# The slots' weights of a graph kernel's last layer in a PSUM bank of their own

## The reference

```
s = x @ msg_w[:, :D].T
d = x @ msg_w[:, D:].T
messages = gelu(s[:, None, :] + d[None, :, :] + msg_b)
aggregated = einsum('ijd,ij->id', messages, adj)
new = concat([x, aggregated], -1) @ upd_w.T + upd_b
h = gelu(new) + x
out = (h - mu) / sqrt(var + eps) * ln_w + ln_b
```

## Time and profile before

| | |
|---|---|
| median of the runs | 754.19 us |
| profiled execution, first to last instruction (span; no other time of that execution is recorded) | 758.7 us |
| busy: TensorE, VectorE, ScalarE, GpSimd | 461.8, 505.2, 302.4, 376.7 us |
| the last layer's pairs | from about 448 us to the end |

### The profile page before, as it was taken

How to read it: one execution, slowest core, us unless ns; L and a number is a source line. 1 busy time by engine, 2 the same in 40 slices (tenths; PEclk the granted TensorE clock), 3 DMA queues, 4 the chain that set the end, 5 groups by cost and what they waited for, 6 DMA issues and landing times.

```text
span 758.7 us, 6873 instructions
## 1 busy us (share of the span) xinstructions
PE 461.8 (61%) x1987; PEld 273.2 (36%) x1987; DVE 505.2 (67%) x1592; ACT 302.4 (40%) x362; POOL 376.7 (50%) x499
## 2 busy tenths in 40 slices
PE   5222016999959999999994586545524642484111
PEld 4121013444425565454463464333313431342110
DVE  2509806998944547983344845999797779777744
ACT  2665255457742331898553230132323222322213
POOL 7204610766650303763003746577777777776640
PEclk9555555899989999999998569677656665655555
DMA  8999992999940202799002221111122122212200
GB/s 325 353 425 419 397 381 39 368 415 390 392 186 0 74 0 76 283 404 421 13 14 78 73 71 49 31 52 49 52 52 56 45 55 54 55 46 56 52 15 14
DMA packets 33212, 120.07 MB, mean 158 GB/s; under 512 B 8704, under 2 KB 19892, under 8 KB 24148
## 3 DMA queue, kind: packets, MB, share of 16 engines
q1 hardware_dynamic: 20258, 80.99, 27.1%
q0 software_dynamic: 10176, 38.57, 16.3%
q10 hardware_dynamic: 2734, 0.01, 0.2%
HBM read 114.00 MB, written 5.55 MB: 158 GB/s over the span
## 4 chain that ended last, share of the span: by engine, by line
PE 34%; POOL 22%; DMA 20%; issue 11%; DVE 6%; ACT 3%; another core or an unknown queue 1%; SPq 1%; ACTq 0%; POOLq 0%
PE ps L121 33%; DMA ring<-in_adjT_dram 18%; POOL G L919 17%; POOL Go L919 5%; DMA G<-near,IX 2%; ACT binT L1001 1%; PE ps L1257 1%; PE ps L1263 1%; DVE M L1703 1%; SPq L822 0%; DVE X L1696 0%; DVE E L1797 0%; ACTq L1004 0%; DVE st L1687 0%
## 5 line engine op out<-in xcount | busy, mean ns | idle before, releaser
L919 POOL DMA_INDIRECT G<-near,IX x154 | 159.6, 1036 | 58.3 <-issue 49.7
L121 PE MATMUL ps<-ring,hwu 128*128 128x512 f32 (+3 forms) x264 | 114.8, 588 | 1.0 <-ACT hwu L1014 1.0
L121 PE MATMUL ps<-ring,xT_s 128*128 128x512 f32 (+2 forms) x264 | 106.9, 547 | 2.0 <-DMA ring<-in_adjT_dram 2.0
L121 PE MATMUL ps<-ident,agg 128*128 128x128 f32 (+1 forms) x44 | 15.9, 461 | 135.6 <-DVE agg L1827 105.2
L1503 DVE FIND_INDEX8 I<-V,rows 128x8 uint32<-128x340 f32 (+2 forms) x176 | 88.1, 504 | 0.0
L1513 DVE MAX8 V<-rows 128x8 f32<-128x340 f32 (+2 forms) x176 | 85.5, 496 | 0.8
L121 PE MATMUL ps<-E,M 128*128 128x321 f32 (+2 forms) x192 | 65.6, 502 | 22.8 <-DVE IO L1719 15.3
L121 PEld LDWEIGHTS ps<-ring,hwu 128*128 128x128 f32 (+1 forms) x264 | 51.4, 204 | 64.4 <-issue 63.3
L1001 ACT ACTIVATE binT<-ring 128x2708 bf16<-128x2708 f32 (+1 forms) x22 | 53.9, 2457 | 44.1 <-DMA ring<-in_adjT_dram 44.1
L942 POOL DMA_DIRECT2D rows<-in_adj_dram x18 | 10.9, 603 | 120.6 <-DVE I L1503 120.6
L1021 ACT ACTIVATE binT<-ring 128x2708 bf16<-128x2708 f32 (+1 forms) x22 | 54.0, 2456 | 37.5 <-PE ps L121 28.4
(11 more groups left out here) (255 smaller groups left out, 859.1 us busy)
## 6 DMA issues: line engine op xcount, KB each, us to landing
ring<-in_adjT_dram SPq DMA_DIRECT2D x48, 1354.0 KB, 16.9
rows<-in_adj_dram POOLq DMA_DIRECT2D x17, 1354.0 KB, 10.2
rows<-in_adj_dram SPq DMA_DIRECT2D x4, 1354.0 KB, 23.4
G<-near,IX POOLq DMA_INDIRECT x154
xT_s<-in_xT_dram SPq DMA_DIRECT2D x1, 1354.0 KB, 6.6
near<-hwu SPq DMA_DIRECT2D x1, 1344.0 KB
out_dram<-yo SPq DMA_DIRECT2D x21, 64.0 KB
near2f<-hwu SPq DMA_DIRECT2D x5, 256.0 KB
```

The source lines that it names most:

```text
L121: return pe.matmul(dst, lhsT, rhs, start=start, stop=stop, skip_group_check=True)
L919: pool.indirect_dma_start(out=dst, out_offset=None, in_=table, in_offset=bass.IndirectOffsetOnAxis(ap=index, axis=0), engine_sem=o_g).then ...
```

## The change

The weights `T8` are copied once by ScalarE, before the pairs begin, into PSUM bank 2, and the multiply in `aggregate` reads them there. Bank 2 held the own shares of every third pair; these now take turns on banks 0 and 1. The share of pair g+1 is made in pair g (from g = 1), at the place in TensorE's order at which that of g+2 stood. The first two shares are made ahead of the pairs, as before. It waits for `features(g-1)`, the last reader of its bank, which is the same wait (`c_h` at g in pair g) as before.

```
--- before.py
+++ after.py
@@ -42,6 +42,7 @@
 MSLOTS = 10
 SUMS = 7 - CAP
 LEAD3 = 3
+SLOT_BANK = 2
 
 
 PAIRS = 11
@@ -258,6 +259,7 @@
         acc = ps[:, 6 * BANK:6 * BANK + D]
         trn = ps[:, 6 * BANK + D:6 * BANK + 2 * D]
         prj = ps[:, 7 * BANK:8 * BANK]
+        slot_weights = bank(SLOT_BANK, 0, NB * 8).rearrange("p (n k) -> p n k", k=8)
         list_bank = ps[:, (8 - CAP) * BANK:8 * BANK].rearrange("p (k e) -> p k e", e=BANK)
         threes = [(q, min(3, GP - q)) for q in range(0, GP, 3)]
 
@@ -290,6 +292,7 @@
         c_hw, c_sg, c_w, c_hws, c_zs = sem("c_hw"), sem("c_sg"), sem("c_w"), sem("c_hws"), sem("c_zs")
         c_acc, c_std, c_x, c_xT, c_hw1, c_pr = sem("c_acc"), sem("c_std"), sem("c_x"), sem("c_xT"), sem("c_hw1"), sem("c_pr")
         c_neg, c_dinv, c_d = sem("c_neg"), sem("c_dinv"), sem("c_d")
+        c_slots = sem("c_slots")
         c_msg, c_msgo, c_aggS, c_h = sem("c_msg"), sem("c_msgo"), sem("c_aggS"), sem("c_h")
 
         v_few, v_set, v_wa, v_u3, v_w2a, v_e, v_w3 = (sem("v_few"), sem("v_set"), sem("v_wa"), sem("v_u3"), sem("v_w2a"),
@@ -1140,6 +1143,9 @@
                 act.activation(pd3[0:r, b, 0:D], bank(g % 2, 0, count * D)[0:r, :].rearrange("p (q w) -> p q w", w=D),
                                ACT.Copy).then_inc(c_d, 1)
 
+            act.wait_ge(v_win, 1)
+            act.activation(slot_weights, T8[:, :, :], ACT.Copy).then_inc(c_slots, 1)
+
             def messages(n):
                 act.wait_ge(v_pre, n + 1)
                 at = G3[0:rn(n), n % QUEUE3, :, :]
@@ -1159,7 +1165,7 @@
                 act.wait_ge(p_nf, g + 1)
                 if g:
                     act.wait_ge(v_h, g)
-                act.activation(hh[:, :, :], bank(g % 3).rearrange("p (b w) -> p b w", w=2 * D)[:, :, D:2 * D], ACT.Gelu).then_inc(c_h, 1)
+                act.activation(hh[:, :, :], bank(g % 2).rearrange("p (b w) -> p b w", w=2 * D)[:, :, D:2 * D], ACT.Gelu).then_inc(c_h, 1)
 
             def deviations3(g, first=0, last=2):
                 for k in range(first, last):
@@ -1394,14 +1400,14 @@
 
             def own_shares(g):
 
-                if g >= 3:
-                    pe.wait_ge(c_h, g - 2)
+                if g >= 2:
+                    pe.wait_ge(c_h, g - 1)
                 if g < NG3 - 1:
-                    last = mm(pe, bank(g % 3), ident[:, :], E2[:, 2 * g:2 * g + 2, EDGE:EW], True, True)
+                    last = mm(pe, bank(g % 2), ident[:, :], E2[:, 2 * g:2 * g + 2, EDGE:EW], True, True)
                 else:
                     for i in range(2):
                         n = 2 * g + i
-                        last = mm(pe, bank(g % 3, i * 2 * D, 2 * D)[0:rn(n), :], ident[0:rn(n), 0:rn(n)], E2[0:rn(n), n, EDGE:EW], i == 0, True)
+                        last = mm(pe, bank(g % 2, i * 2 * D, 2 * D)[0:rn(n), :], ident[0:rn(n), 0:rn(n)], E2[0:rn(n), n, EDGE:EW], i == 0, True)
                 last.then_inc(p_pr, 1)
 
             def own_shares_listed():
@@ -1430,7 +1436,7 @@
                 pe.wait_ge(c_aggS, g + 1)
                 for i in range(2):
                     n = 2 * g + i
-                    at = bank(g % 3, (2 * i + 1) * D, D)[0:rn(n), :]
+                    at = bank(g % 2, (2 * i + 1) * D, D)[0:rn(n), :]
                     last = mm(pe, at, aggS[:, g % 2, i * P:i * P + rn(n)], u2T_s[:, :], False, True)
                 last.then_inc(p_nf, 1)
 
@@ -1446,8 +1452,8 @@
                 aggregate_listed(g)
                 aggregate(2 * g)
                 aggregate(2 * g + 1)
-                if g + 2 < NG3:
-                    own_shares(g + 2)
+                if 0 < g < NG3 - 1:
+                    own_shares(g + 1)
                 new_features(g)
             pe.wait_ge(s_bad, 1)
             mm(pe, prj[:, 0:1], ones[:, :], bads[:, :], True, True).then_inc(s_bad, 1)
@@ -1811,7 +1817,7 @@
 
             def before_gelu(n):
                 r, q = rn(n), n % QUEUE3
-                own = bank(n // 2 % 3, n % 2 * 2 * D, D)[0:r, :]
+                own = bank(n // 2 % 2, n % 2 * 2 * D, D)[0:r, :]
                 dve.wait_ge(p_pr, 2 * CH + n // 2 + 1)
                 dve.tensor_tensor(G3[0:r, q, TOP, :], pd3[0:r, n, 0:D], own, ALU.add)
                 dve.wait_ge(s_g[q], past2[q] + 16 * TOP * (n // QUEUE3 + 1))
@@ -1821,7 +1827,9 @@
             def aggregate(n):
                 r, at = rn(n), G3[0:rn(n), n % QUEUE3, :, :]
                 dve.wait_ge(c_msg, n + 1)
-                few.done(dve.tensor_tensor(at, at, T8[0:r, n, :].unsqueeze(2).broadcast_to([r, TOP + 1, D]), ALU.mult))
+                if n == 0:
+                    dve.wait_ge(c_slots, 1)
+                few.done(dve.tensor_tensor(at, at, slot_weights[0:r, n, :].unsqueeze(2).broadcast_to([r, TOP + 1, D]), ALU.mult))
                 if n >= 2:
                     dve.wait_ge(p_agg, n - 1)
                 dve.tensor_reduce(agg[0:r, n % 2, :], at.rearrange("p k d -> p d k"), AX.X, ALU.add).then_inc(v_agg, 1)
```

## The result

The changed kernel takes 744.77 us (median of 4 runs, 741.12 to 746.34) against 754.19 us (753.02 to 755.95): 0.988 of the time before, interval 0.9848 to 0.9912. Forecast were 743.6 us.

A forecast was written before the change was run, and what follows sets the result against it. GpSimd's gather queue was taken as the bound. Savings of 1.7 + 1.6 + 6.2 + 1.1 = 10.6 us, with the profile's 4.5 us distance to the runs carried over, gave 754.19 - 10.6 = 743.6 us, range 740.8 to 747.0.

The forecast's parts named there:

- (a): GpSimd's gathers after 479.36 us: 18 are stretched by the multiply L1824, and their 12.61 us of surplus goes.
- (b): Steady pairs: moved gathers meet other VectorE instructions, the period falls from 25.54 to 24.3 us, saving 6.2 us over five.
- (c): The other pairs save 1.7, 1.6 and 1.1 us; with the steady pairs' 6.2 the sum is 10.6 us.
- the rule: A gather beginning at least 0.04 us after a tensor_tensor with both inputs in SBUF stands until that one ends.
- (d): The multiply L1824 on VectorE: reading weights from PSUM makes it neither longer nor shorter; cost 0, bounds 0 and 1.0 us each.
- (e): ScalarE's copy of the weights, before the first Gelu: hidden under a wait of 30.52 us, cost 0.
- (f): TensorE's own shares on two banks: the lead before L1816 shrinks to 1.66 us, cost 0.
- The slower rival: VectorE waits at L1816 for TensorE's late own share, or multiplies lengthen over 1.76 us: 761 us; chance 0.04.

The follow-up runs named there:

- e2: The changed kernel with ScalarE's copy of the weights put in an SBUF tile, which the multiply reads: 751.78 us, ratio 1.001.
- e3: The kernel before with the multiply written as scalar_tensor_tensor, both inputs in SBUF: 752.15 us, ratio 1.0002.
- e4: The changed kernel with the two additions before the Gelu reading the own share from E2 in SBUF: 761.41 us, ratio 1.0139.
- e5: The changed kernel without any edit, run again on a second chip: 781.83 us, ratio 1.0183.
- e12: The changed kernel, GpSimd also waiting from pair 2 for the last block's rows before a pair's list gathers, second chip: 766.09 us, ratio 1.0069.
- e7: The changed kernel with take_list working on the lists' PSUM banks directly, without the copy to SBUF, second chip: 777.40 us, ratio 1.0181.
- e11: The changed kernel with e7's edit, and the new features' Gelu and t3 also kept in PSUM, second chip: 778.32 us, ratio 1.0222.

## Why the prediction was right, and where it was not

*The bound and the cause.* What the change gained comes from the weights' move to PSUM. Shown by e2: one tile moved from PSUM to SBUF gives the whole gain back. Shown by e3: a second form of instruction with two SBUF inputs does it too. Shown by e4: an instruction that held nothing holds gathers once its second input is in SBUF. Of the two sentences of the Trainium skill weighed there (SBUF — State Buffer, "Who interferes with whom"), the one on two SBUF inputs holds, and the inferred one by which tensor_tensor leaves descriptor writing alone does not for these indirect gathers (1.99 us against 0.94).

*The sum.* (a) 12.6 us of surpluses beside the multiply are gone, all of them. (b) A steady pair was forecast at 24.3 us with 0.24 beside L1752 and 0.13 beside L1714; it is 24.31 with 0.26 and 0.17. VectorE's wait was forecast at 2.3 and is 2.27. (c) From pair 1 to the last gather the gain is 10.0 against 10.6. All surpluses together fell from 14.9 to 4.0 us, 10.9; what is missing to that is that GpSimd's own odd gap of 1.32 us in place of 0.30, seen once before (at 715.70), came twice (at 599.24 and 697.71). Two readings of (c) were slightly wrong: of the surpluses of 0.09 us beside L1714 there are seven and not six, and a gather at 718.19, held by 0.38 us beside L1810, is missing. The limit of 0.04 us in the rule is not sharp either: over all traces, of gathers that began 0.02 to 0.06 us after an instruction with two SBUF inputs some were held and some were not, and all that began later within it were. (d) The multiply: 1214 ns against 1216. (e) The copy took 0.29 us under a wait of ScalarE of 24 us. (f) The own share was waited for once, 1.35 us at pair 10, where VectorE then waits for rows anyway:

```profile
700.25 0.29 DVE L1822 TENSOR_TENSOR G<-pd,ps 128x128 f32<-128x128 f32 x1 [1.35 <-PE ps L122]
...
706.48 1.09 DVE L1824 TENSOR_TENSOR G<-G,ps 128x896 f32<-128x896 f32 x1 [5.94 <-DMA G<-near,IX]
```

*What failed.* The step from the profiled span to the runs came out well by luck. I carried 4.5 us over as a fixed distance; the after kernel's profiled execution took 1.7 us more than its span, where I had taken 4.5 us less, and the trace of before held 6.2 us that wait ahead of L1711 had cost. The trace of before thus overstated the time of an ordinary run by about what I took off. That wait stood in the timeline and I passed it by. It is of the kind that e5 to e12 met, on an unknown queue, and no rival of mine had VectorE standing in such waits. The slower rival named L1816's wait for the own share, which is not what made the changed kernel slower on the second chip.

*What stays open.* What the unknown queue carries is not known: theory I, that it is the engine's instructions, was not borne out by the packets in the traces. Why the kernel before escapes all but the first wait on the same chip isn't shown either; its gathers of 1.43 and 1.99 us may be the breaks, which no run tested. And why a tensor_scalar with one tensor input held the gather at 548.30 and spared others that began 0.09 to 0.10 us after it wasn't tried.

## What to carry to other kernels

Where GpSimd begins indirect gathers back to back and bounds the stage, lay its starts over VectorE's instructions, those with two SBUF inputs first, and move one input of the longest to PSUM; then carry one period through with the new phases, since others will be met. Before such a gain is believed, look through the timeline for waits on an unknown queue, time it on more than one chip, and see whether the other engines begin to stand when the stream of gathers gets denser, as here, where pauses in that stream made the changed kernel faster on the second chip (e12 against e5).

## What the runs showed of the hardware that was not expected

- On one chip VectorE stood for up to 22 us in one wait on an unknown queue (21.40 us in e7), and ScalarE for up to 13 (e5), while gathers followed each other. Most of VectorE's above 8 us ended 3 to 5.3 us after the last gather's start; in e11 two ended earlier. Pauses of about 2.4 us a pair, from pair 2 on, took all of them away but the first, ahead of pair 1 (e12).
- The packets of the instruction queues that the traces hold lie outside VectorE's waits (e7: 576.40 and 624.11 around a wait from 590.7 to 605.8).
- The same change was worth -1.2% on one chip and +1.8% on another, though an undisturbed pair gained on both (25.54 to 24.31 us, and 25.55 to 24.66).
- Two instructions with two SBUF inputs back to back hold a gather as one: 2.08 us for a gather that began inside the first, of 0.28 us (e4).
- The hold depends on who begins first, within hundredths of a us: a multiply begun 0.04 us ahead of the gather held it for 1.05 us (e2, e3), while gathers that began 0.02 us after L1703 took 0.94 us (the trace of before).
- An instruction with two SBUF inputs that begins inside a running gather is not lengthened: in the changed kernel L1758 takes 0.40 to 0.42 us there, as elsewhere.
